# Bulk writes to DRAM cut into 33 pieces on GpSimd's queue with two under way; other first-head loads and widenings moved between queues

## The reference

```
q, k, v = (xn @ W.T + b) in 16 heads of 8       # xn is LayerNorm of x, batch 16, 256 tokens
content = (q + u_bias) . k                      # 256 x 256 for each batch and head
position = shift((q + v_bias) . p)              # p: 511 relative positions
attn = softmax((content + position) / sqrt(8))
out = (attn @ v) @ Wout.T + bout
```

## Time and profile before

| what | value |
|---|---|
| median of 3 runs | 1024.83 us (1022.76 to 1026.14) |
| the profiled execution's own time | 1022.87 us |
| its span | 1021.0 us |
| mean granted clock of TensorE | 0.912 of full speed |
| busy | PE 81%, DVE 71%, PEld 59%, ACT 53%, POOL 40% |
| bytes moved by DMA | 47.17 MB |
| projections end on PE (last L1076) | 72.2 us |
| first burst of maxima of head 0 (L1132) | 89.1 us |
| first scores of head 0 (L1159) | 103.9 us |
| scores k = 0 of head 1 | 136.8 us |
| time of a head afterwards | 20.7 us |

### The profile page before, as it was taken

The page is one execution under the profiler, slowest core; times in us unless marked ns, Lnnn a source line. Parts: engine busy times, 40 slices in busy tenths (PEclk is TensorE's granted clock), DMA queues, the critical chain, the costliest instruction groups (busy, mean ns, idle before and its releaser), DMA issues.

```text
span 1021.0 us, 23783 instructions
## 1 busy us (share of the span) xinstructions
PE 823.6 (81%) x9611; PEld 599.3 (59%) x9611; DVE 722.0 (71%) x1458; ACT 537.6 (53%) x985; POOL 410.8 (40%) x473
## 2 busy tenths in 40 slices
PE   2494699999999999975479998999998785257773
PEld 1253578888787878754246655666665474135563
DVE  6976366655555555325778898788787688899994
ACT  3860365767666766345445556566564644313332
POOL 5451724443344334344333235334443127214544
PEclk9696699999999999976599999999999798579998
DMA  8037523432343333631000000000000000000111
GB/s 137 11 76 240 131 54 77 100 84 68 78 100 82 72 73 82 164 84 32 1 1 2 2 1 1 2 1 2 1 2 2 0 1 1 0 1 11 21 22 32
DMA packets 55986, 47.17 MB, mean 46 GB/s; under 512 B 22284, under 2 KB 45012, under 8 KB 55156
## 3 DMA queue, kind: packets, MB, share of 16 engines
q1 hardware_dynamic: 36816, 26.24, 11.3%
q0 software_dynamic: 7424, 13.60, 5.6%
q10 hardware_dynamic: 11636, 5.80, 2.3%
HBM read 30.52 MB, written 12.06 MB: 42 GB/s over the span
## 4 chain that ended last, share of the span: by engine, by line
PE 52%; DVE 27%; DMA 5%; issue 5%; POOL 4%; ACT 4%; SPq 2%; POOLq 0%; DVEq 0%; ACTq 0%
PE PS L1159 12%; PE PS L1276 5%; PE PS L1278 5%; PE PS L1277 5%; PE PS L1163 5%; PE PS L1181 5%; PE PS L1132 5%; PE PS L1134 3%; DVE XX L1559 2%; DVE HB L1953 2%; PE PS L1076 2%; DVE XX L1565 2%; DVE AM L1550 2%; DVE ACC L1945 1%; DVE HQ L2082 1%
## 5 line engine op out<-in xcount | busy, mean ns | idle before, releaser
L1691 DVE TENSOR_REDUCE MX<-PS 128x4 f32<-128x1024 f32 x128 | 156.4, 1224 | 123.0 <-PE PS L1134 122.6
L858 ACT ACTIVATE REG<-PS 128x1024 f32<-128x1024 f32 x128 | 130.2, 1018 | 132.1 <-PE PS L1163 120.9
L1159 PE MATMUL PS<-XX,TB 96*128 96x64 f16 x2048 | 160.9, 247 | 5.8 <-issue 3.9
L683 POOL TENSOR_TENSOR HH<-HB,HH 128x512 f16<-128x512 f32 x64 | 75.5, 1180 | 172.4 <-ACT HH L909 172.4
L1159 PEld LDWEIGHTS PS<-XX,TB 96*128 96x128 f16 x2048 | 121.5, 120 | 34.8 <-issue 13.0
L939 ACT ACTIVATE SG<-PS 128x512 f32<-128x512 f32 x128 | 76.2, 595 | 110.6 <-PE PS L1278 110.3
L1953 DVE SCALAR_TENSOR_TENSOR HB<-PS,SG 128x512 f32<-128x512 f32 x128 | 87.8, 686 | 44.4 <-ACT SG L939 44.3
L1163 PE MATMUL PS<-XX,KC 97*128 97x128 f16 x1024 | 107.5, 228 | 0.0
L1276 PE MATMUL PS<-XH,XX 128*128 128x512 f16 x256 | 98.5, 385 | 10.1 <-DVE HB L1953 9.9
L1277 PE MATMUL PS<-XH,XX 128*128 128x512 f16 x256 | 97.9, 382 | 0.0
L1278 PE MATMUL PS<-XH,XX 128*128 128x512 f16 x256 | 97.8, 382 | 0.0
(11 more groups left out here) (237 smaller groups left out, 1721.2 us busy)
## 6 DMA issues: line engine op xcount, KB each, us to landing
REG<-inverse_sums POOLq DMA_DIRECT2D x60, 128.0 KB, 2.9
KC<-keys_strips SPq DMA_DIRECT2D x16, 192.0 KB
keys_strips<-REG ACTq DMA_DIRECT2D x12, 224.0 KB
R<-in_L_attn_x SPq DMA_DIRECT2D x32, 64.0 KB, 3.6
XX<-NEG ACTq DMA_DIRECT2D x120, 1.0 KB, 2.2
R<-REG POOLq DMA_DIRECT2D x60, 32.0 KB, 2.8
queries_position<-REG ACTq DMA_DIRECT2D x2, 896.0 KB
XX<-queries_position SPq DMA_DIRECT2D x56, 32.0 KB
```

The source lines that it names most:

```text
L858: A(P[jt][:, 1024 * up:1024 * up + 1024].rearrange("p (k x) -> p k x", k=2), ST[u % 2], ACT.Exp).then_inc(exp_done, 1)
L1159: mm(o_pos[:, a], TB[p][0:96, y0:y0 + 128], xp[0:96, 8 * bank + a], start=(a == 0), stop=False, skip_group_check=True)
L1691: nc.vector.tensor_reduce(MX[h % 2][:, :].rearrange("p (r a) -> p r a", r=2)[:, :, 2 * g:2 * g + 2], PS[:, bank:bank + 2, :].rearrange("p ...
```

## The change

The order of the work on three queues changes; the arithmetic, the number of bytes and PE's order stay.

- **Bulk writes.** All move to POOL's queue, as one `keys_high` (832 KB), 12 `keys_strips` (224 KB), 8 `queries_position` (224 KB), then the 12 small content copies of head 1, then 8 `queries_content` (208 or 224 KB) and 4 `queries_position_batched` (208 KB). They begin when the low halves of the keys are there (`stage` 14), behind POOL's NQB copies. A new `bulk` gives them alternately to two semaphores and lets piece n wait for piece n - 2. `bulk_landed(engine, count)` stands where the old waits stood: 13 pieces for u = 0, 21 for u = 4, 29 for the context evacuation, 33 for SP at head 1.
- **SP** issues the dense operands of head 1 ahead of head 0's 12 position copies, and no longer issues head 0's `shift_row`.
- **ACT** issues head 0's 12 content copies, widens head 1 (16 pieces), and issues head 0's `shift_row`, all ahead of its first exponential. They count on `x_in[0]`, so PE's separate wait for them at head 0 is gone.
- **POOL** no longer widens head 1.

```diff
+        X_FIRST, X_LOADS = (16 * (12 + 12 + 2), 16 * (12 + 2)), 16 * (8 + 8 + 2)
+        BULK_K, BULK_QV, BULK_QU, BULK_ALL = 13, 21, 29, 33
+        def bulk_landed(eng, count):
+            eng.wait_ge(bulk_out[0], 16 * ((count + 1) // 2))
+            eng.wait_ge(bulk_out[1], 16 * (count // 2))
...
             dense_content_queries(0)
-            first_position_queries(0, range(4))
             dense_position_queries(1)
             dense_content_queries(1)
-            shift_row(0, 0)
+            first_position_queries(0, range(4))
             maximum_keys(1)
             key_operands(1)
             sp.wait_ge(y_wide[0], 8)
             dense_position_queries(2)
             dense_content_queries(2)
-            shift_row(0, 1)
             first_position_queries(1, range(4))
...
                 if h == 1:
-                    sp.wait_ge(khi_out, 16)
...
-                    sp.wait_ge(qu_out, 32)
+                    bulk_landed(sp, BULK_ALL)
...
+            def bulk(dst, src):
+                n = next(count)
+                if n >= 2:
+                    gp.wait_ge(bulk_out[n % 2], 16 * (n // 2))
+                gp.dma_start(dst, src).then_inc(bulk_out[n % 2], 16)
+            gp.wait_ge(stage, 14)
+            bulk(khi_d[rest, :], NAT[NAT_K][rest, :])
+            for k, part in enumerate((0, 0, 1)):
                 for w in range(4):
+                    bulk(k4_d[2:H, w, k], NAT[NAT_K + part][2 * DH:128, strips[w]])
+            gp.wait_ge(stage, 16)
+            for part in range(2):
+                for cols in strips:
+                    bulk(qv_d[2:H, part, :, cols], NAT[NAT_QV + part][2 * DH:128, cols])
             gp.wait_ge(stage, 24)
-            first_content_queries(0)
-            gp.wait_ge(y_dense[1], Y_FIRST[1])
...
-            first_content_queries(1)
+            for w in range(4):
+                for k, part in enumerate(PARTS):
+                    to = 24 * w + 8 * k
+                    gp.dma_start(XC[1][to:to + 8, strips[w]], NAT[NAT_QU + part][DH:2 * DH, strips[w]]).then_inc(content_first, 16)
             for part, h in ((0, FIRST), (1, 2)):
-                gp.dma_start(qu_d[h:H, part], NAT[NAT_QU + part][DH * h:128, :]).then_inc(qu_out, 16)
-            gp.dma_start(qvb_d[rest, :], NQB[rest, :]).then_inc(qvb_out, 16)
+                for cols in strips:
+                    bulk(qu_d[h:H, part, :, cols], NAT[NAT_QU + part][DH * h:128, cols])
+            gp.wait_ge(batched, 8)
+            for cols in strips:
+                bulk(qvb_d[rest, cols], NQB[rest, cols])
...
             act.dma_start(qu_d[0:FIRST, 0], NAT[NAT_QU][0:FIRST * DH, :]).then_inc(qu_first, 16)
-            act.wait_ge(stage, 14)
-            act.dma_start(khi_d[rest, :], NAT[NAT_K][rest, :]).then_inc(khi_out, 16)
...
+            act.wait_ge(zeroed, 8)
             act.wait_ge(stage, 24)
-            for part in range(2):
-                act.dma_start(qv_d[2:H, part], NAT[NAT_QV + part][2 * DH:128, :]).then_inc(qv_out, 16)
+            for w in range(4):
+                for k, part in enumerate(PARTS):
+                    to = 24 * w + 8 * k
+                    act.dma_start(XC[0][to:to + 8, 1024 * w:1024 * w + 1024],
+                                  NAT[NAT_QU + part][0:DH, 1024 * w:1024 * w + 1024]).then_inc(x_in[0], 16)
+            for half in range(2):
+                widened(1, range(8 * half, 8 * half + 8))
+                shift_row(0, half)
...
                     elif u == 0:
-                        act.wait_ge(khi_out, 16)
-                        act.wait_ge(k_out, 16 * 12)
+                        bulk_landed(act, BULK_K)
                     elif u == 4:
-                        act.wait_ge(qv_out, 32)
+                        bulk_landed(act, BULK_QV)
...
                 elif h == 0:
-                    ve.wait_ge(qu_out, 32)
+                    bulk_landed(ve, BULK_QU)
```

More of the change, by code:

```diff
@@ L261, in adaln_program @@
         t_evac_dve, batched, position_dense = (sem(s) for s in ("t_evac_dve", "batched", "position_dense"))
-        content_first = [sem(f"content_first{h}") for h in range(2)]
+        content_first = sem("content_first")
+        bulk_out = [sem(f"bulk_out{j}") for j in range(2)]
         block = outer.enter_context(nc.Block())
@@ L416, in _ @@
                 maximum_positions(h)
-            def shift_row(n, half):
-                sp.wait_ge(neg_ready, 2 * n + half + 1)
-                row = XC[n % 2][96:97, :].rearrange("p (r m c t a) -> p r c t m a", r=2, m=64, c=2, t=2)
-                for r in range(2):
-                    for c in range(2):
-                        sp.dma_start(row[:, r, c, half], NEG[half][64 * c:64 * c + 64, 8 * r:8 * r + 8]).then_inc(neg_in[half], 16)
             def first_keys(h):
@@ L589, in _ @@
             rest = slice(FIRST * DH, 128)
-            def first_content_queries(h):
-                for w in range(4):
-                    for k, part in enumerate(PARTS):
-                        to = 24 * w + 8 * k
-                        gp.dma_start(XC[h][to:to + 8, 1024 * w:1024 * w + 1024],
-                                     NAT[NAT_QU + part][DH * h:DH * h + DH, 1024 * w:1024 * w + 1024]).then_inc(content_first[h], 16)
-            gp.wait_ge(stage, 24)
-            first_content_queries(0)
@@ L609, in _ @@
-            first_content_queries(1)
-            for part, h in ((0, FIRST), (1, 2)):
-                gp.dma_start(qu_d[h:H, part], NAT[NAT_QU + part][DH * h:128, :]).then_inc(qu_out, 16)
-            gp.dma_start(qvb_d[rest, :], NQB[rest, :]).then_inc(qvb_out, 16)
+            rest, strips = slice(FIRST * DH, 128), [slice(1024 * w, 1024 * w + 1024) for w in range(4)]
+            count = itertools.count()
+            def bulk(dst, src):
[3 more added lines that the diff above has]
+                gp.dma_start(dst, src).then_inc(bulk_out[n % 2], 16)
@@ L836, in _ @@
             act.dma_start(qu_d[0:FIRST, 0], NAT[NAT_QU][0:FIRST * DH, :]).then_inc(qu_first, 16)
-            rest = slice(FIRST * DH, 128)
-            act.wait_ge(stage, 14)
-            act.dma_start(khi_d[rest, :], NAT[NAT_K][rest, :]).then_inc(khi_out, 16)
-            for k, part in enumerate((0, 0, 1)):
-                for w in range(4):
-                    act.dma_start(k4_d[2:H, w, k], NAT[NAT_K + part][2 * DH:128, 1024 * w:1024 * w + 1024]).then_inc(k_out, 16)
-            act.wait_ge(stage, 24)
-            for part in range(2):
-                act.dma_start(qv_d[2:H, part], NAT[NAT_QV + part][2 * DH:128, :]).then_inc(qv_out, 16)
+            act.wait_ge(zeroed, 8)
+            act.wait_ge(stage, 24)
+            for w in range(4):
[6 more added lines that the diff above has]
+                shift_row(0, half)
             for h in range(H):
```

21 lines of the change are left out of this document (5 added, 16 removed).

## The result

| kernel | median us (runs) | ratio to before | profiled execution us | span us |
|---|---|---|---|---|
| before | 1025.68 (15) | 1 | 1022.87 | 1021.0 |
| changed | 1028.33 (15; 1025.31 to 1033.02) | 1.0033 [1.0017, 1.0048] | 1028.07 | 1026.2 |

The account below looks back on a forecast made before the run. DMA, not arithmetic, was taken to bound the stretch before head 1, small loads waiting behind large writes. The smaller of 12.0 (compute path) and 9.6 us (last bulk landing) gave 1015.2 from 1024.83; range 1011.5 to 1022.5.

Parts of the forecast that it names:

- the compute path: From first burst to PE's k = 4 in head 1: 102.6 us where it was 114.65, 12.0 us earlier.
- term 4: Bulk writes on POOL's queue: 3.1 us a piece, last landing at 127.9, so head 1 at most 9.6 us earlier.
- Term 1: First burst of head 0: quicker content-query write and dense content rows let PE start near 84.9, 4.2 us earlier.
- the early part does not move: Rival: small loads stay late, first burst stays at 89.1, a gain of 7.8 us remains, 1017.0; chance 0.1.
- Term 2: Head 0's first scores: with ACT issuing shift_row they begin near 95.8 instead of 103.86.
- Term 3: Head 1's wide operands: ACT widens them, PE's 3.28 us wait goes, k = 4 comes at 102.6, not 114.65.
- the dear wait: SP's wait at L467 for the last bulk write, ahead of head 3's dense rows; limits head 1's gain to 9.6 us.
- The rule against the sum: Bulk pieces: the skill page's fit gives 2.5 us for 224 KB instead of 3.1, so the chain would not bind.
- The quick case: Rival: pieces take 2.9 us or less, writes land before 125.5, all 12.0 us remain, 1012.8; chance 0.2.
- the second rival: Bulk pieces take 3.3 to 3.9 us, each 0.1 us costing 1.5; at 3.5 it is 1021.2; chance 0.2.
- the third: Rival: from 3.75 us a bulk piece, ACT's queue stalls and head 1 comes later than before; chance 0.05.

Follow-up runs that it names:

- e1: Changed kernel with four bulk pieces under way instead of two; ratio 0.9998 to the kernel before.
- e5: Changed kernel with keys_high started only when head 0's dense content rows have landed, and four pieces under way; ratio 0.9906 to the kernel before.
- e7: As e5, with the writes that head 3's dense rows need ahead of queries_content part 1, SyncE waiting for 29 pieces; ratio 0.9897.
- e15: As e7, but GpSimd waits only for head 0's dense position rows, so keys_high starts 2.6 us earlier; ratio 0.9914.
- e13: The changed kernel again, unaltered, for a second profiled execution; ratio 1.0043 to the kernel before.
- e2: Changed kernel with queries_position_batched pieces ahead of queries_content part 1, SyncE waiting for 29 pieces, not 33, before head 3's dense loads; ratio 0.9999.
- e12: Changed kernel with the late start of e5 alone, still two pieces under way; ratio 1.0068 to the kernel before.
- e4: Changed kernel with ACT's first write of content queries cut into three DMAs, one for each head; ratio 1.0034 to the kernel before.
- e6: Changed kernel with the old 18 unbounded bulk writes, the keys' thirteen on ACT's queue, all else of the change kept; ratio 1.0138 to the kernel before.
- e11: Changed kernel with the late start of e5 and no bound on the pieces under way; ratio 1.0072 to the kernel before.

## Why the prediction was wrong, step by step

**Which step decided the time.** The forecast took the smaller of two gains, 12.0 by the compute path and 9.6 by the last bulk landing. So the step that failed for the time is term 4: its 3.1 us a piece. By the text's own count (15 pieces behind the first, 7.4 for the copies) the measured chain is (73.0 - 7.7 - 7.4) / 15 = 3.86 us a piece, and the last landing comes 68.6 behind the origin, where 127.9 meant 55.9. Term 1 failed as well, and with it goes the gain that is left once the stall is gone (e1).

**Term 1, the first burst, is the step that failed first in the order of time.** The text took `keys_high` to start at 67.7 in the middle of SyncE's issues, and then said of the position rows' widening "I leave them there". They landed 5.6 us later behind the origin (means of two executions each) and carried the burst with them: 2.2 later instead of 4.2 earlier. The rival "the early part does not move" came nearest, and had nothing where 2.2 later was measured. The write of the content queries, forecast to shrink from 5.67 us to 4.3, took 10.1, since `keys_high` ran beside it. The content rows landed 3.33 us after their issue, as forecast (3), but so late that they alone would have left the burst where it was: 14.4 behind the origin in both kernels. With the start moved (e5, e7, e15) the burst is 3.9 us earlier, 13.1 against 17.0; there the write takes 5.8 us, so the gain is in the rows themselves, 2.0 to 2.5 us for 7.8. The sum had a slip too: with the position rows left at 78.98, DVE has 6.1 us of work until the last widening (6.25 in e5 from its first widening to the burst), which gives 85.2 and not 84.9, and the bound of 83.2 could not be reached. I had costed the new position of the writes for what they do to each other and not for the queue that they now run beside.

**Term 2, right in kind.** From first burst to first scores it was 14.8 us before; forecast 10.9, measured 11.8 in the changed kernel and 12.4 in e7. ACT's shift rows are no longer late, but four NEG issues took 3.0 us and landed at 100.4.

**Term 3, right in sign, too large.** The compute path was to win 12.0. Head 1 comes 4.8 us earlier behind the origin in the changed kernel (mean of two) and 8.6 on the mean of e5, e7 and e15, so 3.4 of the 12.0 were not there even with term 1 made good. The first scores account for 2.2 of it (5.9 earlier in these three, where 8.1 were forecast). The other 1.2 goes between the first scores and head 1. PE's granted clock does not explain it: it is 0.50 from 90 to 100 us in the kernel before too.

**Term 4, the dear wait, failed in its size.** 3.1 us a piece was right for the quiet second half only: 2.62 to 2.85 for the landing and 0.28 to the next issue. In the first half the ten steps from 72.66 to 114.15 cost 4.15 each, and the first piece 7.72, not 6.3. A single price for all, drawn from a quiet 16 KB round trip, hid that half the pieces run in the traffic of the other queues. The high bound of the text, 3.55, was too low as well; by its own terms the bounds are 122.1 and 135.5, not 122.4 and 135.7. Of the 12.7 us by which the landing came later behind the origin, 1.4 are the first piece and 10.5 the nine steps behind it (4.27 for 3.1 each).

**The price of the stall was too low.** The text's threshold of 137.5, in the clock of the kernel before, is 65.5 behind the origin; the landing at 68.6 should by it cost 3.1 us. Head 2 came 7.5 and 5.5 us later behind the origin. From landing to dense rows 4.7 us were right (4.8 forecast). The text then took another 2.3 us of slack between ACT and PE, 0.8 more than ACT idles there. From u = 1's exponential to head 2 it is 18.2 us in the kernel before (141.6 to 159.8), less the 1.45 that ACT idles there: 16.7. Measured are 20.3 (144.3 to 164.6) and 18.8 (e13, 146.1 to 164.9), 3.6 and 2.1 more. This fits PE's clock, which fell while PE waited. The changed kernel, from 140 to 160 us (PE, PEld, DVE, ACT, POOL; then clock, DMA share, GB/s):

```profile
140.00:150.00 10.00, 4.68 (x50) 4.14 (x51) 1.23 (x1) 6.64 (x13) 7.26 (x8) 0.61 0.33 91
150.00:160.00 10.00, 10.00 (x142) 7.66 (x141) 5.29 (x13) 4.73 (x9) 0.53 (x2) 0.71 0.10 24
```

In the kernel before the granted clock is 1.00 in both stretches. So this stall cost its own length and then some 2 to 4 us at the lower of the two levels, 1.2 instead of 2.4 GHz: the eight matmuls of L1162 take 1.04 us there and 0.62 before the stall.

**What carries the loss.** Head 1 starts 4.8 us earlier and head 2 6.5 later behind the origin; ACT's stall is the difference. e1 and e2 remove it or most of it and the loss is gone; e12 makes the early part good and keeps the stall, and stays slower; e5, e7 and e15 remove both causes and win 0.9 to 1.0%, what had been forecast for the change itself.

**The rule against the sum.** It stood for quicker pieces. The rows show 2.6 to 2.9 us for a piece where little else moves and up to 8.3 where SyncE and ACT issue. The page of the Trainium skill, "DMA: Bandwidth & Descriptors" (section "Anatomy of one DMA — SWDGE (gpsimd) path"), fits 2.0 us plus bytes / 436 GB/s, an estimate of 2.5 us for 224 KB. In the quiet the trace nearly agrees, beside other queues it does not.

The section "Queues, rings and completion order" of that page of the Trainium skill says that a DMA engine takes turns between the queues that have work, packet by packet. I would read it so that a small load hardly cares how many pieces stand in GpSimd's queue. The traces do not bear that reading out: the position rows landed 18.9 us behind the origin without a bound and 13.1 with two under way, the content rows at 32.1 and 14.4.

**The other rivals.** The quick case (2.9 us a piece or less) is out. The mean of 3.86 us lies at the upper end of the second rival (3.3 to 3.9) and past the 3.75 of the third, "two under way are too few, and ACT's queue turns that into a stall", which had a chance of 0.05. Its mechanism is the one that came. Its own sum gives 1024.83 + 3.1 = 1027.9 for this landing, and the median is 1028.33. That the two agree so closely is partly luck: the stall cost more than the text's price, and the ratio moved by less than head 2 did.

**Open.** Why the position rows took 9 us in the changed kernel with the DMA engines busy to 0.51 and 0.56:

```profile
76.00:80.00 4.00, 0.66 (x6) 0.47 (x5) 0.00 (x0) 0.00 (x0) 0.00 (x0) 1.00 0.51 146
80.00:84.00 4.00, 0.00 (x0) 0.00 (x0) 1.55 (x3) 0.00 (x0) 1.13 (x2) 0.59 0.56 150
```

The share is a mean over 16 engines. The same page of the Trainium skill (section "Why a DMA increments its semaphore by 16 and not by 1") says that a DMA runs on the largest number of engines, up to 16, that divides the outer count of both its sides, and on SyncE's and ACT's queues on the lowest-numbered ones. No run here shows the engines apart. ACT's copies have 8 rows, so half the engines may be full while the mean is a half; but the same copies run in e7, where the rows took 5.8 us, and e4, which spreads ACT's first write differently, gained only about 0.8 us. So unevenly filled engines could count only together with the bulk pieces, and this stays open, as do the 1.2 us between first scores and head 1.

## What to carry to other kernels

A bound on the bulk writes under way protects small loads only from what comes behind; it says nothing on where the writes begin. Ask first which small load gates the next stage, and start the bulk behind its issue; then choose the depth so that the last write lands before its first reader needs it, and no deeper, since four pieces under way cost some 3 us more than two in the early part. Price a chain of round trips by the traffic of each stretch, and a stall of PE at its length plus the time that it runs slowly afterwards. And compare early stages from an event that the edit does not move.

## What the runs showed of the hardware that was not expected

- Issuing gets slower, not only landing. An issue of 224 KB on ACT's queue took 2.30 us (27.54 / 12 in e6), one of a 1 KB row 2.1 (8.42 / 4 in e11), with the DMA engines 0.74 to 0.98 busy in e6 and full in e11 (a share of 1.01 from 92 to 101 us); in the changed kernel issues of 1 KB rows take 0.62 at 101 to 103 us (2.50 / 4), at a share of 0.60. In e11 ACT hands out only small DMAs and is held while the large ones are on GpSimd's queue.
- The mean DMA share does not tell how late a small load lands. The position rows, 64 KB, took 5.9 us at a share of 0.74 in the kernel before (73 to 79 us), 9.2 at 0.54 in the changed kernel (73 to 82), and 13.3 at 0.99 without a bound (76 to 90).
- A first piece of 832 KB takes 7.7 us beside SyncE's early transfers and 5.6 once they are gone (e7, e12, e15).
